# Expert results of a two-expert mixture: stored as pairs and combined in a last stage, or weighted and added in memory by an accumulating scatter

## What is computed

```python
h = layernorm(x) * (1 + cb) + sb
xf = h                                  # tokens x 256
w, idx = top_k(xf @ Wg, 2);  w = softmax(w)
xhat = (xf - mean) * rsqrt(var + eps)
out_e = relu((xhat * gamma_e + beta_e) @ W1_e + b1_e) @ W2_e + b2_e + xf   # for the two experts picked
y = sum over the two picks of w * out_e
result = x + gb * y                     # gb: one row of 256 numbers per sequence
```

## Time and profile before

| | us |
|---|---|
| median of 3 runs | 1849.6 (1848.32 to 1850.16) |
| the profiled execution, its own time | 1847.45 |
| its span in the trace | 1845.4 |
| stage A | 0 to 1212 |
| stage B | 1212 to 1257 |
| stage C | 1257 to 1794 |
| stage D | 1794 to 1845.4 |

### The profile page before, as it was taken

The page is one execution under the profiler, slowest core; times in us unless marked ns, Lnnn a source line. Parts: engine busy times, 40 slices in busy tenths (PEclk is TensorE's granted clock), DMA queues, the critical chain, the costliest instruction groups (busy, mean ns, idle before and its releaser), DMA issues. The chain is left out here.

```text
span 1845.4 us, 27287 instructions
## 1 busy us (share of the span) xinstructions
PE 1344.8 (73%) x7872; PEld 1093.0 (59%) x7873; DVE 1316.3 (71%) x2414; ACT 903.1 (49%) x1326; POOL 967.5 (52%) x857
## 2 busy tenths in 40 slices
PE   2666777676677676676676666558999999999970
PEld 0244555454465454454454554447999999999960
DVE  1397998998897998997998999473444444444438
ACT  2567667667557657657657565122222222222200
POOL 2287768767668768768758778101222222222210
PEclk6788898898797898898898888757999999999985
DMA  4211111301311311311201311045711111111118
GB/s 123 86 52 58 34 36 35 109 35 36 105 41 36 105 39 36 108 36 36 91 25 36 91 35 66 3 138 166 239 37 34 38 36 34 40 34 37 37 48 291
DMA packets 81351, 124.65 MB, mean 68 GB/s; under 512 B 8728, under 2 KB 51224, under 8 KB 81120
## 3 DMA queue, kind: packets, MB, share of 16 engines
q1 hardware_dynamic: 69280, 99.02, 16.8%
q0 software_dynamic: 6912, 18.88, 3.2%
q10 hardware_dynamic: 5056, 5.56, 0.9%
HBM read 96.91 MB, written 26.53 MB: 67 GB/s over the span
## 5 line engine op out<-in xcount | busy, mean ns | idle before, releaser
L442 POOL TENSOR_TENSOR dBu<-u,brep 128x512 f32<-128x512 f32 x512 | 650.2, 1301 | 115.2 <-DVE hs L966 65.4
L966 DVE TENSOR_TENSOR_SCAN hs<-psum,dBu 128x512 f32<-128x512 f32 x512 | 608.9, 1210 | 68.9 <-ACT psum L589 59.4
L762 PE MATMUL psum<-ident,hs 128*128 128x128 f32 x2048 | 323.8, 309 | 206.0 <-DVE y L977 160.9
L589 ACT ACTIVATE psum<-dt,aneg 128x512 f32<-128x512 f32 x512 | 347.6, 688 | 232.0 <-DVE hs L966 228.2
L762 PEld LDWEIGHTS psum<-ident,hs 128*128 128x128 f32 x2048 | 261.7, 159 | 292.8 <-DVE y L977 214.0
L1380 ACT ACTIVATE w_now<-w_sb 128x2048 f32 x72 | 137.5, 1910 | 382.6 <-PE psum L1401 373.3
L1401 PE MATMUL psum<-xgT,w_now 128*128 128x128 f32 x2304 | 270.9, 276 | 0.0
L771 PE MATMUL psum<-ident,hc 128*128 128x128 f32 x1024 | 186.1, 315 | 113.6 <-ACT hc L575 74.5
L1401 PEld LDWEIGHTS psum<-xgT,w_now 128*128 128x128 f32 x2304 | 265.0, 193 | 0.1
L1362 POOL DMA_INDIRECT y_d<-ysb,row_of_y x72 | 71.1, 987 | 369.0 <-DVE ysb L1459 362.5
L1412 PE MATMUL psum<-w_sb,hT 128*128 x1152 | 260.4, 379 | 0.0
(11 more groups left out here) (159 smaller groups left out, 1327.6 us busy)
## 6 DMA issues: line engine op xcount, KB each, us to landing
brep<-b_d SPq DMA_DIRECT2D x128, 256.0 KB, 3.2
w_sb<-in_W SPq DMA_DIRECT2D x16, 1024.0 KB
y<-y_d SPq DMA_DIRECT2D x8, 1024.0 KB, 7.7
xin<-in_x SPq DMA_DIRECT2D x8, 512.0 KB, 7.2
h_d<-hmod SPq DMA_DIRECT2D x8, 512.0 KB, 3.0
modo<-mod_d SPq DMA_DIRECT2D x8, 512.0 KB, 5.7
xres<-in_x SPq DMA_DIRECT2D x8, 512.0 KB, 6.8
hres<-h_d SPq DMA_DIRECT2D x8, 512.0 KB, 7.6
```

The source lines that it names most:

```text
L442: nc.gpsimd.tensor_tensor(dBu[:, i % RING, :], u[:, p, c, :], brep[:, s % 4, :], ALU.mult).then_inc(s_dBu, 1)
L589: nc.scalar.activation(dA[:, i % DA_RING, :], dt[:, p, c, :], ACT.Exp, scale=aneg[:, c, s:s + 1]).then_inc(s_dA, 1)
L762: last = nc.tensor.transpose(T[:, i // DT, c * P:(c + 1) * P], hs[:, s % 2, c, i * P:(i + 1) * P], ident[:, :])
L966: nc.vector.tensor_tensor_scan(hs[:, s % 2, c, :], dA[:, i % DA_RING, :], dBu[:, i % RING, :], 0.0, ALU.mult, ALU.add).then_inc(s_scan, 1)
```

## The change

The base is stored into `sum_d`, and each slot's results are added onto it by a scatter that accumulates, so that `sum_d` holds the output when the last slot has landed. Stage D is gone; SP and ACT copy `sum_d` to `out`, memory to memory, four blocks of 512 rows each.

For that each slot needs the pair's weight and gb. They travel with the token: a row of `xhat_d` grows from 256 to 514 numbers (xhat, the two weights, gb), so SP makes three stores per sequence instead of one, and the first of them waits for `s_scaled`. Stage B makes two masks `pick0` and `pick1` (which of the two weights a pair uses; both 0 for a filler), and fillers now add zeros to 128 spare rows, which are zeroed at the start. In stage C, DVE makes `weight` from the two numbers and the masks (two operations on 128x1) and multiplies ysb by weight and gb (one on 128x256). A scatter waits until the one before it has landed, since two slots may hold the same token. `xg` now has a reader that comes late (the multiplication by gb), so gather(j+4) waits for `ysb` of j and stands behind scatter(j).

```diff
-    y12_d = dram("y12_d", (1 + 2 * NTOK + NSLOT * P, D))
+    xhat_d = dram("xhat_d", (NTOK, XW))            # XW = D + 2 + D
+    sum_d = dram("sum_d", (NTOK + P, D))
 # stage A, SP
             def store_xhat(n):
+                sp.wait_ge(s_scaled, n + 1)
+                sp.dma_start(part(D, 2), wts[:, bass.ds(n * TI, TI), :]).then_inc(s_xhst, 16)
+                sp.dma_start(part(D + 2, D), modo[:, 3, :].unsqueeze(1).to_broadcast([P, TI, D])).then_inc(s_xhst, 16)
                 sp.wait_ge(s_xh, n + 1)
-                sp.dma_start(rows(xhat_d, n), xh[:, :, :]).then_inc(s_xhst, 16)
+                sp.dma_start(part(0, D), xh[:, :, :]).then_inc(s_xhst, 16)
 # stage B, DVE, behind row_x
+            link(nc.vector.tensor_scalar(pair[:, :], pair[:, :], 1, None, ALU.bitwise_and))
+            link(nc.vector.tensor_copy(pick1[:, :], pair[:, :]))
+            nc.vector.scalar_tensor_tensor(pick0[:, :], PLACE, 0.0, pick1[:, :], ALU.is_gt, ALU.subtract)
+            link(nc.vector.tensor_copy(token[:, :], row_x[:, :]))
 # stage C, POOL
             def gather(j):
-                after(pool, s_xtp, j - XR + 1)
+                after(pool, s_ys, j - XR + 1)
             def scatter(j):
                 pool.wait_ge(s_ys, j + 1)
-                pool.indirect_dma_start(y12_d, ..., ysb[:, j % YR, :], None)
+                if j > 0:
+                    pool.wait_ge(s_st[(j - 1) % YR], 16 * ((j - 1) // YR + 1))
+                pool.indirect_dma_start(sum_d, ..., ysb[:, j % YR, :], None, compute_op=ALU.add)
             for j in range(NSLOT):
+                scatter(j)
                 if j + XR < NSLOT:
                     gather(j + XR)
-                scatter(j)
 # stage C, DVE: x_in and y_in
+                nc.vector.tensor_scalar(weight[:, r:r + 1], xg[:, r, D:D + 1], pick0[:, bass.ds(j, 1)], None, ALU.mult).then_inc(s_pick, 1)
+                nc.vector.scalar_tensor_tensor(weight[:, r:r + 1], xg[:, r, D + 1:D + 2], pick1[:, bass.ds(j, 1)], weight[:, r:r + 1],
+                                               ALU.mult, ALU.add).then_inc(s_weight, 1)
+                nc.vector.scalar_tensor_tensor(ysb[:, r, :], ysb[:, r, :], weight[:, r:r + 1], xg[:, r, D + 2:XW],
+                                               ALU.mult, ALU.mult).then_inc(s_ys, 1)
 # end, on SP (even n) and ACT (odd n)
+                eng.dma_start(out[n * L:(n + 1) * L, :].rearrange("(p i) d -> p (i d)", p=P),
+                              sum_d[n * L:(n + 1) * L, :].rearrange("(p i) d -> p (i d)", p=P)).then_inc(s_out, 16)
-def stage_d(...)
```

More of the change, by code:

```diff
@@ L39 @@
 EARLY = 2
-BASES = 4
+XW = D + 2 + D
 YR = 4
@@ L85, in adaln_kernel @@
         YT = psum[:, 4:8, :]
-        stage_a(nc, ctx, sem, ident, oh, wts, T, dA, Q, MOD_PS, YT, mod_d, b_d, h_d, xhat_d, base_d,
+        stage_a(nc, ctx, sem, ident, oh, wts, T, dA, Q, MOD_PS, YT, mod_d, b_d, h_d, xhat_d, sum_d,
                 x, norm_w, W_in, conv_w, conv_b, W_x, W_dt, b_dt, A_log, D_skip, W_out, Wg, cT, wmod)
[L89 to L92, removed]
         with ExitStack() as held:
@@ L101, in adaln_kernel, with stage_a @@
             s_we = sem("expert_weights_loaded")
-            stage_b(nc, sem, oh, row_x, row_y, tile_expert, psum,
+            stage_b(nc, sem, oh, row_x, row_y, pick0, pick1, tile_expert, psum,
                     w1_sb, w2_sb, b1_sb, b2_sb, gam, bet, W1, W2, b1, b2, gamma, beta, weights_in, s_we)
[L104 to L109, removed]
+            stage_c(nc, sem, ident, row_x, row_y, pick0, pick1, tile_expert, psum, xhat_d, sum_d, out, w1_sb, w2_sb, b1_sb, b2_sb,
+                    gam, bet, W1, W2, s_we)
+def stage_a(nc, ctx, sem, ident, oh, wts, T, dA, Q, MOD_PS, YT, mod_d, b_d, h_d, xhat_d, sum_d,
             x, norm_w, W_in, conv_w, conv_b, W_x, W_dt, b_dt, A_log, D_skip, W_out, Wg, cT, wmod):
@@ L330, in store_base @@
                 sp.wait_ge(s_base, n + 1)
-                sp.dma_start(rows(base_d, n), x1[:, :, :]).then_inc(s_bast, 16)
+                sp.dma_start(rows(sum_d, n), x1[:, :, :]).then_inc(s_bast, 16)
             def prologue():
@@ L336, in prologue @@
                 store_h(0)
+                sp.wait_ge(s_const, 1)
+                sp.dma_start(sum_d[NTOK:NTOK + P, :], zrow).then_inc(s_zero, 16)
                 store_h(1)
@@ L597, in o_xhat @@
                 act.wait_ge(s_ln3r, n + 1)
-                after(act, s_xhst, 16 * n)
+                after(act, s_xhst, 48 * n)
                 normalise(xh, xf, 2).then_inc(s_xh, 1)
@@ L1326, in stage_c @@
         s_ys = sem("ysb_ready")
-        s_st = [sem(f"y_stored{i}") for i in range(YR)]
+        s_yb = sem("y_with_bias")
+        s_pick = sem("first_weight_picked")
+        s_weight = sem("weight_ready")
+        s_st = [sem(f"y_added{i}") for i in range(YR)]
+        s_out = sem("out_stored")
         block = own.enter_context(nc.Block())
@@ L1333, in after, with store_out @@
                 eng.wait_ge(s, value)
+        def store_out(eng, parts):
+            for r in range(YR):
+                eng.wait_ge(s_st[r], 16 * (NSLOT // YR))
+            for n in parts:
+                eng.dma_start(out[n * L:(n + 1) * L, :].rearrange("(p i) d -> p (i d)", p=P),
+                              sum_d[n * L:(n + 1) * L, :].rearrange("(p i) d -> p (i d)", p=P)).then_inc(s_out, 16)
         def tiles(eng, body):
@@ L1347, in _ @@
                 sp.wait_ge(s_we, 16 * (k + 1))
[L1348 to L1351, removed]
+            store_out(sp, range(0, NB, 2))
+            sp.wait_ge(s_out, 16 * NB)
         @block.gpsimd
@@ L1382, in _ @@
             tiles(act, step)
+            store_out(act, range(1, NB, 2))
         @block.tensor
@@ L1409, in second @@
                 pe.wait_ge(s_ht, j + 1)
-                after(pe, s_ys, j - 1)
+                after(pe, s_yb, j - 1)
                 for k in range(FC):
```

100 lines of the change are left out of this document (28 added, 72 removed).

## The result

| | before | after |
|---|---|---|
| median, us | 1849.3 (4 runs, 1848.32 to 1850.16) | 1823.92 (4 runs, 1820.82 to 1826.33) |
| ratio | | 0.9867 (0.9855 to 0.9878) |
| profiled execution, span, us | 1845.4 | 1821.0 |

The change makes the kernel 1.3% faster; the forecast was 1827.4 us, in a range of 1813 to 1860. A second series of the changed kernel gave 1824.58 us, ratio 0.9859 (0.9843 to 0.9874). One execution of a later experiment took 3851 us in the slow state, and the median given there leaves it out. The two traces differ by 24.4 us, and they can be cut at the same events: the start of stage B, the first gather, PE's first transposes, those of the thirteenth slot (the weights have been loaded by then), the last transposes, and the last y_in.

A forecast was written before the change was run, and what follows sets the result against it. PE was taken to bound stage C, while stage D left it idle. Terms -30.0 (end), +6 (turns beside weight loads), +0.5, +0.95 and +0.4 sum to -22.2 us, from 1849.6 to 1827.4, range 1813 to 1860.

The forecast's parts named there:

- The end: From the last y_in on: stage D replaced by a copy with 20 us of data, -30.0 us.
- The quiet turns: Stage C once the weights are loaded: gathers land in time, turns stay at 7.25 us, cost 0.
- slack of 1.0 us: Stage C, quiet turns: a gather has 4.2 us from start to landing and takes 3.2.
- rival 1: Stage C: gather late every turn, 30 us per us of lateness; chance 0.12 slightly late, 0.15 strongly late.
- The scatter's data: Stage C: the adding scatter's extra read of 128 KB, 0.36 us, is covered and costs nothing.
- Beside the weight loads: Stage C up to 1330: late gathers cost 0.4 to 1.3 us on some 8 turns, +6 us.
- DVE, 0: Stage C: three added operations per slot, about 0.95 us, fit into 2.05 us of idle time, cost 0.
- The chain of scatters: Stage C: each scatter waits for the one before, landing in 3.5 us against 6.9 allowed, cost 0.
- Rival 2: Stage C: scatter landings over 6.9 us set the turn; at 8 us, 75 us more, 1902; chance 0.06.
- Stages A and B: Before stage C: end of A +0.5 us, four more operations in B +0.95, first gather's doubled data +0.4.
- rival 4: Stage A pays for late brep loads, 3 us on 7 sequences, giving 1848 us; chance 0.03.
- rival 3: Final copy slow because transfers are cut into 16 long pieces: 42 us at 100 GB/s, 1849; chance 0.06.

The follow-up runs named there:

- halving experiment: Changed kernel with only four of the eight blocks copied to the output, the other half left out: 1815.42 us, ratio 0.9822 to the kernel before.
- rings of six: Changed kernel with six instead of four buffers for gathered rows and results, gathers issued two turns earlier: 1814.54 us, ratio 0.9814 to the kernel before.
- The order alone: Kernel before, with only gather(j+4) waiting for ysb of j and standing behind scatter(j): 1851.5 us, ratio 1.0017.
- the experiment that removes the cause in part: Changed kernel with six buffers instead of four and stage A's token-row stores issued behind the last brep load: 1816.24 us, against 1814.54 without that move.

## Why the prediction was right, point by point

**The verdict and the size.** -24.4 us in the traces, -25.4 in the medians, -22.2 forecast. The mechanism was the one named: stage D goes, PE's turns pay a little. But the sum came out so near by luck in part: the end was 6.2 us better than forecast, the quiet turns and stage A 2.8 and 2.0 us worse.

**The end, -30.0, measured -36.2.** The term that was wrong is the copy. I had 20 us of data, near the slow bound, 2.8 fixed and 0.5 to the span's end, 23.3 in all; it is 16.0, some 14.4 of data and 1.6 fixed. Its rate is 290 GB/s in the halving experiment, between the bounds of 395 and 195 that the rows gave. I leaned to the slow end because no row showed a byte crossing memory twice; the middle of the two bounds, 16 us of data, would have been nearer. The Trainium skill's figure that I had set beside it ("DMA: Bandwidth & Descriptors", section "Latency and other measured facts", 207 to 214 GB/s between HBM tensors, in tiles with a wide row pitch) is not what this copy does: the measurement decides. The last scatter started 1.4 us after its data were ready, where I had said it wouldn't be held: its predecessor landed after 3.8 us and not 3.5, and POOL started 0.75 us after that. So the copy was issued 1.1 us later than forecast.

**The quiet turns, 0, measured +2.8 (1.9 in the second trace).** The deciding step was the slack of 1.0 us. DVE's multiplication (0.49) and POOL's reaction (0.27) were right. Two things were missed: POOL needs 1.59 us for an adding scatter, a duration for which I took the plain one's 0.99 without a bound, and the landing was 3.4 and not 3.2. A third is small: 0.12 us and not 0.03 between DVE's two dependent operations (1598.79 to 1598.91). 1.0 - 0.6 - 0.2 - 0.1 leaves 0.1 us, and every landing above 3.5 us is late. So rival 1 in its slight form came true; its price, half a lateness per turn, would need a mean lateness of 0.1 us for 2.8 us over 60 turns, which fits the two turns shown, with 0.18 and 0.31 us of idle time ahead of the transposes. The experiments put the cost where the rival put it: it is gone with the gather ahead, with a plain scatter, or with rings of six.

**The scatter's data.** I had held a read of 0.36 us against the plain scatter's 0.36 and called the sum covered. It takes 1.0 us of the engines against 0.4, a factor of 2.6. By the rule of two source reads (the Trainium skill, "Collectives: The Full Stack", section "The bandwidth ceiling", a ratio of 1.93) an estimate is 0.7 to 0.8 us: right in direction, too small here. Its packets end 3.0 to 3.3 us after the scatter's start, about when the gather's begin; that they delay the gather isn't shown, since the landing is 3.3 with plain scatters as well.

**Beside the weight loads, +6, measured +5.2 and 8.0.** The size is right, within the bounds of 3 to 10 (4.9 to 10.1 over four traces), and the cause, gathers that land late, is the one named. The way there was not, so the size is luck in part. I had every one of eight turns late by half of 0.8 to 2.6 us; in the four traces one to three gathers are late by 2 to 3 us and the others by little or nothing, and a term that I didn't have, the lower clock, adds 1.6 us (5.37 against 3.74) behind one of them in three of the four traces. The order alone made 3.3 us in its one trace.

**DVE, 0.** Right in the turns, by rings of six: its operations are there and the stretch of stage C is as long as before within 0.7 us.

**The chain of scatters, 0.** Right: landing after 3.8 us against 6.9 that a turn allows. Rival 2 had no part.

**Stages A and B.** B's +0.95 was +0.9, the first gather's +0.4 was +0.5. POOL does wait for brep and the ring covers it: rival 4 had no part, by the 1.1 us that DVE waited in all and by the experiment that removes the cause in part and gains nothing. Stage A grew by 2.5 us, not 0.5. Of that 1.4 is at its end. SP's rows there, last store and first load of stage B, first of the changed kernel:

```profile
1210.08 0.37 SPq L336 DMA_DIRECT2D sum_d<-x  x1
1214.86 0.38 SPq L1124 DMA_DIRECT2D w_sb<-in_W  x1
```

and with rows of 1032 bytes, where the store of gb is left out:

```profile
1206.12 0.38 SPq L335 DMA_DIRECT2D sum_d<-x  x1
1209.53 0.38 SPq L1123 DMA_DIRECT2D w_sb<-in_W  x1
```

4.78 us against 3.41; before it was 3.41 too (1208.96 to 1212.37). The base store queues behind the store of gb. The remaining 1.1 is no effect that I can show: stage B starts anywhere from 1210.8 to 1215.7 in seven traces with the changed stage A (1214.0 on average), and at 1212.4 and 1213.2 in the two with that of before.

**The slow copy (rival 3).** No part: 16.0 us in pieces of 32 KB, 15.9 in pieces of 1 KB.

## What to carry to other kernels

When a ring's last reader moves later, price the refill as a chain from that reader to the next use, with the issuing engine's own time for every transfer that it now stands behind; here 0.1 us of slack cost 2 to 3 us over 59 quiet turns and 5 to 10 us beside the weight loads. Two more buffers gave back all but 0.7 us of it, one swap of issue order all of the quiet part. The accumulating scatter paid for itself here because it removed a stage in which the matrix engine was idle (1.3%), and more so when it added onto the output itself, with unused rows dropped by a bounds check, so that no copy was left (2.5%, with rings of six). A term that has only bounds from far rows had better be taken in the middle; of that the copy is one case.

## What the runs showed of the hardware

An indirect scatter of 128 rows of 1 KB that adds in memory costs POOL 1.59 us to issue (plain 0.99), keeps the 16 DMA engines busy for 1.0 us (0.4) and lands 3.8 us after its start (2.4), all by the experiment that stores instead of adding. An indirect gather of 128 rows lands after 2.8 us with rows of 1024 or 1032 bytes and after 3.4 with 2056. A copy from memory to memory in pieces of 32 KB ran at 290 GB/s, and took as long in all in pieces of 1 KB (15.9 us against 16.0), where loads into and stores from the chip together reached 390. After a wait of 2.46 us for a gather, PE's granted clock was 0.50 in the following product, which took 5.37 us and not 3.74; after waits of 2.18 and 2.49 us in another trace it stayed at 1.00.
